# Block product as three float32r terms, with the transposed x1 split by ScalarE and VectorE

## The chip, the cores and the metric

The program runs on one core of a Trainium2 chip. Its engines are TensorE (PE; its weight loads are shown apart as PEld), VectorE (DVE), ScalarE (ACT), GpSimd (POOL) and SyncE (SP, which only starts transfers here). Each engine works through its own queue in order, and the engines meet at semaphores. The metric is the device time of one execution in microseconds (us); lower is better.

## What is computed

For each of 128 batches (128 tokens of 256 features), a layer norm is followed by cross attention with 16 heads against a context, a residual sum (x1), a second layer norm, and a feed-forward step in which a router keeps 96 of the 128 tokens and sends them through one 256x256 matrix and a gelu.

```python
def attn(q_in, ctx):                     # 16 heads of 16
    q = q_in @ Wq + bq
    k, v = split(ctx @ Wkv + bkv)
    return (softmax(q @ k.T / 4) @ v) @ Wo + bo
x1 = x + attn(layernorm(x), ctx)         # x: [128, 128, 256], float32
h = layernorm(x1)
score = h @ w_router                     # top 96 of 128 tokens in each batch
out = x1 + where(token is kept, gelu(h @ w_block), h)
```

## The kernel before

**Tiling.** One batch is one tile of 128 tokens on 128 partitions, so each of the 128 steps of the main loops handles one batch per stage. The code is written engine by engine, with the order of every queue written out by hand. Several batches are in flight: in step s, PE computes the scores of batch s, transposes the inputs of batch s+5, and runs the block product (h @ w_block and the router column together, `w_z_sb`, 258 columns) of batch s-4.

**PE, step s** (loop at the end of the tensor block): `scores(s)`, `transpose_inputs(s+5)`, `values(s-1)`, queries or keys of a later pair, on two steps of eight a small router transpose, `projection(s-2)`, `block_product(s-4)`, `transpose_x1(s-3)`, `attention(s-1)`. The weight matrices for q, k and v stand as a float32r high part and a low part, and `three_terms` multiplies them as hi·hi + hi·lo + lo·hi (six matmuls of 256 columns for two halves of the contraction). `projection` and `block_product` go through `full_terms`: two float32 matmuls, each of which the trace shows as two records.

**ACT, step s**: `attention_copy(s-2)` (PSUM to `o_sb`, 256 columns), `gelu_tanh(s-7)`, `inputs_high(s+5)` (the 512-column cast of the transposed inputs to float32r, L578), then the exponentials of batch s in the order j = 3, 2, 1, 0. Each j is four ACTIVATEs of 128 columns with an accumulated sum, so a batch has sixteen, each followed by a record that reads the accumulator.

**DVE, step s**: `x1_transposed(s-4)` (copy of the transposed x1 from PSUM to `xt_sb`, L721), layer-norm statistics, router steps, `maxima(s, 3)` and `(s, 2)`, value bias, `inputs_low`, reciprocal of the sums, `maxima(s, 1)`, query or key bias, residual sum, `maxima(s, 0)`, the final sum of an older batch, and `product_scaled(s-4)`, which reads the block product.

**What ties them.** `scores(s)` waits until ACT has done j = 1 of batch s-1 (`exp_ready[1]`), because they share PSUM banks; only the bank of j = 0 alternates. `inputs_high(s+5)` waits for the transposes behind `scores(s)` (`t_mm`). The exponentials (s, j) wait for the maxima (s, j), and these for the scores. `values(s-1)` waits for `attention_copy(s-2)`. The transposed x1 lies in the bank that queries and keys use next (`ps_q`), and those wait for the copy out of it (`xt_ready`).

**The tail.** After the last step the remaining batches drain. There ACT also does five `unprocessed` steps in a row (L602, batches B-13 to B-9), and DVE runs `gelu_product(B-5)`, which needs ACT's tanh of that batch, ahead of `product_scaled(B-2)`.

Of the kernel before, what the change touches and what calls it, by code (L numbers as in the profile page):

```python
# [6 lines left out]
def cross_attention_routed_ffn(  # L7
# [14 lines left out]
    f32 = mybir.dt.float32  # L22
    f32r = mybir.dt.float32r
# [7 lines left out]
    P = 128  # L31
# [16 lines left out]
    with ctx:  # L48
        def sb(name, shape, dt=f32):
            return ctx.enter_context(nc.sbuf_tensor(name, shape, dt))  # L50

        def sem(name):
            return ctx.enter_context(nc.semaphore(name))
# [14 lines left out]
        x1_sb = sb("x1_sb", [P, R, E])  # L68
        xt_sb = sb("xt_sb", [P, 2, E])
        z_sb = sb("z_sb", [P, R, ZW])  # L70
# [3 lines left out]
        w_o_sb = sb("w_o_sb", [P, C, E])  # L74
        w_z_sb = sb("w_z_sb", [P, C, ZW])
        bq_sb = sb("bq_sb", [P, C])
        bk_sb = sb("bk_sb", [P, C])
# [56 lines left out]
        def has(b):  # L134
            return 0 <= b < B

        def upto(b):
            return min(b + 1, B)
# [17 lines left out]
        w_lo_ready = {n: sem(f"w_{n}_lo_ready") for n in "qkv"}  # L156
        w_mean_mm, w_z_ready = sem("w_mean_mm"), sem("w_z_ready")
        st1_ready, mv1_ready, ve1_ready, rstd1_ready = sem("st1_r"), sem("mv1_r"), sem("ve1_r"), sem("rstd1_r")
        st2_ready, mv2_ready, ve2_ready, rstd2_ready = sem("st2_r"), sem("mv2_r"), sem("ve2_r"), sem("rstd2_r")
# [21 lines left out]
        x1_ready = sem("x1_ready")  # L181
        xt_mm = sem("xt_mm")
        xt_ready = sem("xt_ready")
        z_mm = sem("z_mm")
# [93 lines left out]
        def _(pe):  # L278
# [17 lines left out]
            def full_terms(dst, lhs, rhs):  # L296

                for c in range(C):
                    last = nc.tensor.matmul(dst, lhs(c), rhs(c), start=(c == 0), stop=(c == C - 1))  # L299
                return last  # L300
# [123 lines left out]
            def block_product(b, settled=False):  # L424

                if not has(b):
                    return
                if not settled:
                    pe.wait_ge(xt_ready, upto(b))
                pe.wait_ge(t_lo_ready, upto(b + 9))  # L430
                if has(b - 1) and not has(b + 9):
                    pe.wait_ge(z_ready, upto(b - 1))
                full_terms(ps_z,
                           lambda c: xt_sb[:, b % 2, c * T:(c + 1) * T],
                           lambda c: w_z_sb[:, c, :]).then_inc(z_mm, 1)

# [114 lines left out]
        def _(act):  # L551
# [4 lines left out]

            def exps(b, j, settled=False):

                if not has(b):
                    return  # L560
                act.wait_ge(max_ready[j], upto(b))
                if j == 3 and has(b - 4) and not settled:
                    act.wait_ge(a_mm, upto(b - 4))
                for c in range(C):
                    for par in range(2):
                        h = c * 2 * J + 2 * j + par
                        last = nc.scalar.activation(e_sb[:, b % 4, j, c, par, :], ps_s[:, bank(b, j), c, par, :], ACT.Exp,  # L567
                                                    bias=neg_max[:, b % 4, h:h + 1],
                                                    accum_out=sums[:, b % 4, h:h + 1])
                last.then_inc(exp_ready[j], 1)  # L570

# [73 lines left out]
            exps(1, 1)  # L645
            exps(1, 0)

            for s in range(2, B):
                sure = 20 <= s < B - 1
                attention_copy(s - 2, sure)  # L650
                gelu_tanh(s - 7)
                inputs_high(s + 5, sure)
                exps(s, 3, sure)
                exps(s, 2)
                exps(s, 1)
                exps(s, 0)

            attention_copy(B - 2)
            gelu_square(B - 5)
            gelu_tanh(B - 7)  # L660
            gelu_square(B - 4)
            attention_copy(B - 1)
            gelu_tanh(B - 6)
            for b in range(B - 13, B - 8):
                unprocessed(b)
# [12 lines left out]
        def _(dve):  # L678
# [35 lines left out]

            def x1_transposed(b, settled=False):

                if has(b):
                    dve.wait_ge(xt_mm, upto(b))
                    if has(b - 2) and not settled:
                        dve.wait_ge(z_mm, upto(b - 2))  # L720
                    nc.vector.tensor_copy(xt_sb[:, b % 2, :], ps_xt).then_inc(xt_ready, 1)  # L721

# [190 lines left out]
            for s in range(2, B):  # L913
                sure = 20 <= s < B - 1
                x1_transposed(s - 4, sure)
                if s >= 4:
# [35 lines left out]
            router(B - 16, 8)  # L952
            x1_transposed(B - 4)
            aggregate2(B - 3)
            router(B - 16, 9)
            inverse_sums(B - 1)
            router(B - 16, 10)
            x1_transposed(B - 3)
            product_scaled(B - 4)
# [5 lines left out]
            final(B - 15)  # L965
            x1_transposed(B - 2)
            gelu_product(B - 6)
# [3 lines left out]
            product_scaled(B - 3)  # L971
            x1_transposed(B - 1)
            final(B - 14)
# [236 lines left out]
```

## Time and profile before

| | |
|---|---|
| three runs, us | 920.46, 921.12, 921.23 (median 921.12) |
| profiled execution: its span, first to last instruction | 919.4 us |
| median of the runs less that span | 1.7 us |
| busy share of the span: PE, PEld, DVE, ACT, POOL | 97%, 82%, 95%, 96%, 87% |
| mean DMA rate | 77 GB/s |

The page gives the span of one profiled execution; what lies around it is the 1.7 us by which the median of the other runs is longer. Busy shares are averages: three engines are above 94%, so they do not say by themselves which one sets the pace. For that one reads a single batch in the timeline, engine beside engine, and looks for who starts right behind whom.

### The profile page before, as it was taken

To read this page: it belongs to the slowest core of one execution; us is meant where nothing else is said; L and a number is where in the kernel's file an instruction comes from. 1 tells how busy PE (TensorE), PEld (TensorE's weight loads), DVE (VectorE), ACT (ScalarE), POOL (GpSimd) and SP (SyncE) were. 2 spreads that over 40 slices of the span, in tenths; PEclk is the share of its full clock that TensorE was granted. 3 is DMA by queue.
4 is the path that set the end of the run, shared out by engine and by line. 5 is a ranking of instruction groups with operands and counts; after the bars stand their busy time and mean duration, and the time that the engine had idled before them with its cause. 6 is when DMAs were issued, how large, how long until landed. Compare 5 with 4: busy or idle time off the path is not lost. (4 is left out here: it accounts for less than half of the span.)

```text
span 919.4 us, 31003 instructions
## 1 busy us (share of the span) xinstructions
PE 889.4 (97%) x10306; PEld 753.9 (82%) x10306; DVE 873.5 (95%) x2320; ACT 879.5 (96%) x4503; POOL 796.8 (87%) x1488
## 2 busy tenths in 40 slices
PE   7899999999999999999999999999999999999973
PEld 6788888888888888888888888888888888888861
DVE  6899999999999999999999999999999999999887
ACT  5999999999999999999999999999999999999983
POOL 4568789999989999899999999999899999998865
PEclk9999999999999999999999999999999999999997
DMA  6222123223223223223223223223223222221102
GB/s 198 62 65 71 46 61 95 57 84 93 57 84 95 60 83 92 58 86 91 70 75 91 59 86 91 71 74 89 76 71 89 76 71 87 76 61 53 49 24 92
DMA packets 70976, 70.45 MB, mean 77 GB/s; under 512 B 12064, under 2 KB 62752, under 8 KB 70816
## 3 DMA queue, kind: packets, MB, share of 16 engines
q1 hardware_dynamic: 69456, 67.68, 25.5%
q8 instruction: 82, 1.34, 0.6%
q10 hardware_dynamic: 1360, 0.79, 0.3%
q14 instruction: 78, 0.64, 0.2%
HBM read 35.13 MB, written 16.78 MB: 56 GB/s over the span
## 5 line engine op out<-in xcount | busy, mean ns | idle before, releaser
L567 ACT ACTIVATE e_sb<-ps_s,neg_max 128x128 f32<-128x128 f32 x2048 | 719.1, 411 | 4.4 <-DVE neg_max L712 3.9
L567 ACT ACTIVATION_READ_ACCUMULATOR e_sb<-ps_s,neg_max 128x1 f32 x2048 | 513.5, 251 | 0.0
L712 DVE TENSOR_REDUCE neg_max<-ps_s 128x4 f32<-128x512 f32 x512 | 329.0, 663 | 26.4 <-PE ps_s L337 26.4
L337 PE MATMUL ps_s<-q_eo,k_sb 32*128 32x256 f32 x2048 | 146.6, 400 | 1.1 <-DVE k_sb L790 0.5
L402 PE MATMUL ps_a<-e_sb,v_pad 128*32 128x128 f32 x4096 | 138.4, 276 | 2.2 <-DVE x_sb L729 1.6
L299 PE MATMUL ps_a<-w_o_sb,o_sb 128*128 128x256 f32 x512 | 133.2, 382 | 2.0 <-DVE v_sb L803 1.9
L299 PE MATMUL ps_t<-w_z_sb,xt_sb 128*128 128x258 f32 x512 | 132.6, 381 | 1.3 <-DVE z_sb L815 1.3
L1042 POOL TENSOR_TENSOR v_pad<-v_sb,recip 128x256 f32<-128x256 f32 x128 | 79.6, 622 | 54.0 <-DVE recip L757 52.5
L402 PEld LDWEIGHTS ps_a<-e_sb,v_pad 128*32 128x32 f32 x4096 | 104.1, 109 | 24.0 <-issue 21.6
L337 PEld LDWEIGHTS ps_s<-q_eo,k_sb 32*128 32x128 f32 x2048 | 92.5, 184 | 29.4 <-ACT e_sb L567 17.0
L1031 POOL TENSOR_TENSOR x_sb<-x_sb,bo_sb 128x256 f32<-128x256 f32 x128 | 114.0, 892 | 0.2
L299 PEld LDWEIGHTS ps_t<-w_z_sb,xt_sb 128*128 128x128 f32 x512 | 97.3, 191 | 15.4 <-issue 1.8
L299 PEld LDWEIGHTS ps_a<-w_o_sb,o_sb 128*128 128x128 f32 x512 | 88.0, 189 | 10.1 <-issue 2.4
L1088 POOL TENSOR_TENSOR g_sb<-g_sb,z_sb 128x256 f32<-128x256 f32 x128 | 90.9, 710 | 0.3
L578 ACT CAST t_hi<-ps_t 128x512 fp32r<-128x512 f32 x126 | 74.2, 589 | 14.0 <-PE ps_t L366 10.5
L764 DVE TENSOR_TENSOR t_lo<-ps_t,t_hi 128x512 fp32r<-128x512 f32 x126 | 85.2, 676 | 1.4 <-ACT t_hi L578 1.4
L292 PE MATMUL ps_a<-w_v_hi,t_hi 128*128 128x256 f32 x256 | 84.4, 330 | 1.7 <-ACT o_sb L586 1.6
L1102 POOL TENSOR_TENSOR z_sb<-g_sb,z_sb 128x256 f32<-128x256 f32 x121 | 82.8, 685 | 0.0
L1071 POOL TENSOR_TENSOR g_sb<-z_sb 128x256 f32<-128x256 f32 x123 | 75.6, 614 | 0.3 <-DVE z_sb L815 0.3
L292 PE MATMUL ps_q<-t_hi,w_k_hi 128*128 128x256 f32 x252 | 71.2, 282 | 1.6 <-DVE q_raw L777 1.6
L292 PE MATMUL ps_a<-w_v_lo,t_hi 128*128 128x256 f32 x256 | 72.5, 283 | 0.0
L292 PE MATMUL ps_q<-t_hi,w_q_hi 128*128 128x256 f32 x256 | 72.3, 282 | 0.2 <-DVE t_lo L764 0.2
(102 smaller groups left out, 2197.6 us busy)
## 6 DMA issues: line engine op xcount, KB each, us to landing
x_sb<-in_x SPq DMA_DIRECT2D x64, 256.0 KB, 2.9
c_sb<-in_ctx SPq DMA_DIRECT2D x64, 256.0 KB, 3.1
out<-z_sb SPq DMA_DIRECT2D x64, 256.0 KB, 2.4
q_eo<-q_raw SPq DMA_DIRECT2D x504, 32.0 KB, 2.0
z_sb<-in_L_xattn_Wkv ACTq DMA_DIRECT2D x2, 256.0 KB, 7.2
z_sb<-in_L_xattn_Wq ACTq DMA_DIRECT2D x1, 256.0 KB, 4.5
w_z_sb<-in_L_ffn_w_block SPq DMA_DIRECT2D x1, 256.0 KB, 7.6
w_o_sb<-in_L_xattn_Wo SPq DMA_DIRECT2D x1, 256.0 KB, 7.0
```

The source lines that it names most:

```text
L292: last = nc.tensor.matmul(dst, lhs(a, c), rhs(b, c), start=(c == 0 and n == 0), stop=(c == C - 1 and n == len(terms) - 1))
L299: last = nc.tensor.matmul(dst, lhs(c), rhs(c), start=(c == 0), stop=(c == C - 1))
L337: mm = nc.tensor.matmul(ps_s[:, bank(b, j), c, :, :], k_sb[rows, r2, c, h * T:(h + 1) * T], q_eo[rows, r2, :, c, h, :], start=True, stop=True)
L402: mm = nc.tensor.matmul(ps_attn[32 * j:32 * j + 32, c * T:(c + 1) * T], v_pad[:, b % 2, c * J + j, par:par + 2, :].rearrange("p a d -> p ( ...
L567: last = nc.scalar.activation(e_sb[:, b % 4, j, c, par, :], ps_s[:, bank(b, j), c, par, :], ACT.Exp, bias=neg_max[:, b % 4, h:h + 1], accu ...
L712: nc.vector.tensor_reduce(neg_max[:, b % 4, :].rearrange("p (c j q) -> p j c q", c=C, j=J)[:, j, :, :], ps_s[:, bank(b, j), :, :, :], AX.X ...
L764: nc.vector.tensor_tensor(t_lo[part].rearrange("p k c t -> p (k c) t"), inputs_bank(b)[:, :].rearrange("p (n t) -> p n t", t=T), t_hi[part ...
L1031: nc.gpsimd.tensor_tensor(x_sb[:, b % R, :], x_sb[:, b % R, :], bo_sb[:, :], ALU.add).then_inc(xb_ready, 1)
L1042: nc.gpsimd.tensor_tensor(v_pad[:, b % 2, :, 0:3:2, :], v_sb[:, b % 2, :].rearrange("p (g q d) -> p g q d", q=2, d=D), recip[:, b % 4, :]. ...
L1071: nc.gpsimd.tensor_tensor(g_sb[:, b % 4, :], z_sb[:, b % R, 0:E], z_sb[:, b % R, 0:E], ALU.mult).then_inc(square_ready, 1)
L1088: nc.gpsimd.tensor_tensor(g_sb[:, b % 4, :], g_sb[:, b % 4, :], z_sb[:, b % R, 0:E], ALU.mult).then_inc(cubic_ready, 1)
L1102: nc.gpsimd.tensor_tensor(z_sb[:, b % R, 0:E], g_sb[:, b % 4, :], z_sb[:, b % R, 0:E], ALU.mult).then_inc(gelu_ready, 1)
```

## The change

The block product goes from `full_terms` to `three_terms`: six float32r matmuls instead of two float32 ones. For that, both operands need a high and a low part. The weights are split once (`block_weights_high` on ACT in step 2, `block_weights_low` on DVE in step 3). The transposed x1 is split in every batch: ACT writes the high part with a new copy (`x1_high`, PSUM to float32r, 256 columns), and DVE subtracts it from PSUM to get the low part (`x1_low`), where it made a plain copy before. `x1_high(s-4)` stands on ACT between j = 1 and j = 0 of batch s-1, and `attention_copy(s-2)` moves from behind those last four exponentials to between their two halves. The diff shows PE's queue first, then ACT's, then DVE's.

```diff
             def block_product(b, settled=False):
...
-                full_terms(ps_z,
-                           lambda c: xt_sb[:, b % 2, c * T:(c + 1) * T],
-                           lambda c: w_z_sb[:, c, :]).then_inc(z_mm, 1)
+                if b == 0:
+                    pe.wait_ge(w_z_lo_ready, 1)
+                three_terms(ps_z,
+                            lambda a, c: (xt_hi, xt_lo)[a][:, b % 2, c * T:(c + 1) * T],
+                            lambda a, c: (w_z_hi, w_z_lo)[a][:, c, :]).then_inc(z_mm, 1)
...
+            def block_weights_high():
+
+                act.wait_ge(w_z_ready, 1)
+                nc.scalar.copy(w_z_hi[:, :, :], w_z_sb[:, :, :]).then_inc(w_z_hi_ready, 1)
+
+            def x1_high(b, settled=False):
+
+                if has(b):
+                    act.wait_ge(xt_mm, upto(b))
+                    nc.scalar.copy(xt_hi[:, b % 2, :], ps_xt).then_inc(xt_hi_ready, 1)
...
-            exps(1, 0)
 
             for s in range(2, B):
                 sure = 20 <= s < B - 1
+                x1_high(s - 4, sure)
+                exps(s - 1, 0, halves=(0,))
                 attention_copy(s - 2, sure)
+                exps(s - 1, 0, halves=(1,))
                 gelu_tanh(s - 7)
                 inputs_high(s + 5, sure)
                 exps(s, 3, sure)
                 exps(s, 2)
                 exps(s, 1)
-                exps(s, 0)
-
+                if s == 2:
+                    block_weights_high()
+
+            x1_high(B - 4)
+            exps(B - 1, 0, halves=(0,))
             attention_copy(B - 2)
+            exps(B - 1, 0, halves=(1,))
+            x1_high(B - 3)
             gelu_square(B - 5)
             gelu_tanh(B - 7)
             gelu_square(B - 4)
             attention_copy(B - 1)
+            x1_high(B - 2)
             gelu_tanh(B - 6)
-            for b in range(B - 13, B - 8):
+            unprocessed(B - 13)
+            unprocessed(B - 12)
+            x1_high(B - 1)
+            for b in range(B - 11, B - 8):
                 unprocessed(b)
...
-            def x1_transposed(b, settled=False):
-
-                if has(b):
-                    dve.wait_ge(xt_mm, upto(b))
-                    if has(b - 2) and not settled:
-                        dve.wait_ge(z_mm, upto(b - 2))
-                    nc.vector.tensor_copy(xt_sb[:, b % 2, :], ps_xt).then_inc(xt_ready, 1)
+            def block_weights_low():
+
+                dve.wait_ge(w_z_hi_ready, 1)
+                nc.vector.tensor_tensor(w_z_lo[:, :, :], w_z_sb[:, :, :], w_z_hi[:, :, :].bitcast(f32),
+                                        ALU.subtract).then_inc(w_z_lo_ready, 1)
+
+            def x1_low(b):
+
+                if has(b):
+                    dve.wait_ge(xt_hi_ready, upto(b))
+                    nc.vector.tensor_tensor(xt_lo[:, b % 2, :], ps_xt, xt_hi[:, b % 2, :].bitcast(f32),
+                                            ALU.subtract).then_inc(xt_ready, 1)
...
-                x1_transposed(s - 4, sure)
+                x1_low(s - 4)
+                if s == 3:
+                    block_weights_low()
```

In the tail of DVE's queue each `x1_transposed(b)` is replaced in its place by `x1_low(b)`.

On ACT, in the middle of the run, this is how one batch's last exponentials stood before, with the waits of each instruction (`e_sb` are the exponentials, `o_sb` the attention output, `g_sb` the gelu's work tile, `t_hi` the inputs' high part):

```order
L567 ACTIVATE e_sb,sums<-ps_s,neg_max 128x128 [waits max_ready1]
L567 ACTIVATE e_sb,sums<-ps_s,neg_max 128x128 x3
L567 ACTIVATE e_sb,sums<-ps_s,neg_max 128x128 [waits max_ready0]
L567 ACTIVATE e_sb,sums<-ps_s,neg_max 128x128 x3
L586 COPY o_sb<-ps_a 128x256 [waits a_mm]
L609 ACTIVATE g_sb<-g_sb 128x256 [waits cubic_ready]
L578 CAST t_hi<-ps_t 128x4x128 [waits t_mm]
```

and this is how they stand now (`xt_hi` is the high part of the transposed x1):

```order
L586 ACTIVATE e_sb,sums<-ps_s,neg_max 128x128 [waits max_ready1]
L586 ACTIVATE e_sb,sums<-ps_s,neg_max 128x128 x3
L573 CAST xt_hi<-ps_q 128x256 [waits xt_mm]
L586 ACTIVATE e_sb,sums<-ps_s,neg_max 128x128 [waits max_ready0]
L586 ACTIVATE e_sb,sums<-ps_s,neg_max 128x128
L606 COPY o_sb<-ps_a 128x256 [waits a_mm]
L586 ACTIVATE e_sb,sums<-ps_s,neg_max 128x128 x2
L629 ACTIVATE g_sb<-g_sb 128x256 [waits cubic_ready]
L598 CAST t_hi<-ps_t 128x4x128 [waits t_mm]
```

One instruction of 256 columns came in ahead of the last four exponentials, and the COPY of `o_sb` moved up by two of them.

On DVE, between two steps, from the statistics of x1 to the first maximum of the next batch, before:

```order
L735 BN_STATS st<-x_sb 128x6 [waits x1_ready]
L815 TENSOR_SCALAR z_sb<-ps_t,rstd 128x258 [waits stored2,z_mm]
L721 COPY xt_sb<-ps_q 128x256 [waits xt_mm]
L746 BN_STATS st<-x_sb 128x6
L740 BN_AGGR mv<-st 128x2 [waits st2_r]
L751 BN_AGGR mv<-st 128x2 [waits st1_r]
L712 TENSOR_REDUCE neg_max<-ps_s 128x2x2 [waits s_mm3]
```

and now:

```order
L771 BN_STATS st<-x_sb 128x6 [waits x1_ready]
L851 TENSOR_SCALAR z_sb<-ps_t,rstd 128x258 [waits stored2,z_mm]
L756 TENSOR_TENSOR xt_lo<-ps_q,xt_hi 128x256 [waits xt_hi_ready]
L782 BN_STATS st<-x_sb 128x6
L776 BN_AGGR mv<-st 128x2 [waits st2_r]
L787 BN_AGGR mv<-st 128x2 [waits st1_r]
L743 TENSOR_REDUCE neg_max<-ps_s 128x2x2 [waits s_mm3]
```

The instruction stands in the same place, but its input now comes from ACT as well (`xt_hi_ready`), where it waited for PE alone (`xt_mm`).

On ACT in the tail, from the last exponentials on, before:

```order
L567 ACTIVATE e_sb,sums<-ps_s,neg_max 128x128 x3
L586 COPY o_sb<-ps_a 128x256 [waits o_mm,a_mm]
L595 ACTIVATE g_sb<-z_sb 128x256 [waits gelu_ready,z_ready]
L609 ACTIVATE g_sb<-g_sb 128x256 [waits cubic_ready]
L595 ACTIVATE g_sb<-z_sb 128x256 [waits gelu_ready,z_ready]
L586 COPY o_sb<-ps_a 128x256 [waits o_mm,a_mm]
L609 ACTIVATE g_sb<-g_sb 128x256 [waits cubic_ready]
L602 ACTIVATE x_sb<-x_sb,beta,alpha 128x256 [waits xt_mm,beta_ready] x5
L609 ACTIVATE g_sb<-g_sb 128x256 [waits cubic_ready]
L595 ACTIVATE g_sb<-z_sb 128x256 [waits gelu_dve_ready,z_ready]
```

and now:

```order
L586 ACTIVATE e_sb,sums<-ps_s,neg_max 128x128 x2
L573 CAST xt_hi<-ps_q 128x256 [waits xt_mm]
L615 ACTIVATE g_sb<-z_sb 128x256 [waits gelu_ready,z_ready]
L629 ACTIVATE g_sb<-g_sb 128x256 [waits cubic_ready]
L615 ACTIVATE g_sb<-z_sb 128x256 [waits gelu_ready,z_ready]
L606 COPY o_sb<-ps_a 128x256 [waits o_mm,a_mm]
L573 CAST xt_hi<-ps_q 128x256 [waits xt_mm]
L629 ACTIVATE g_sb<-g_sb 128x256 [waits cubic_ready]
L622 ACTIVATE x_sb<-x_sb,beta,alpha 128x256 [waits xt_mm,beta_ready] x2
L573 CAST xt_hi<-ps_q 128x256 [waits xt_mm]
L622 ACTIVATE x_sb<-x_sb,beta,alpha 128x256 [waits xt_mm,beta_ready] x3
L629 ACTIVATE g_sb<-g_sb 128x256 [waits cubic_ready]
```

Three of the new copies stand in this stretch, the last of them ahead of three of the five `unprocessed` steps and of the gelu work behind these.

## Rows read from the trace of the kernel before

**Rows 1.** The page's part 1: busy time (share of the span) and instructions of each engine.

```profile
PE 889.4 (97%) x10306; PEld 753.9 (82%) x10306; DVE 873.5 (95%) x2320; ACT 879.5 (96%) x4503; POOL 796.8 (87%) x1488
```

**Rows 2.** Groups by line, ACT: form, count, busy us, mean ns, idle before, releaser.

```profile
L578 ACT CAST t_hi<-ps_t 128x512 fp32r<-128x512 f32 x126 | 74.2, 589 | 14.0 <-PE ps_t L366 10.5
...
L586 ACT COPY o_sb<-ps_a 128x256 f32<-128x256 f32 x128 | 60.2, 470 | 2.2 <-PE ps_a L402 2.2
```

**Rows 3.** Timeline, ACT, one batch: start us, us, line, operation, out<-in.

```profile
502.24 0.26 ACT L567 ACTIVATION_READ_ACCUMULATOR e_sb<-ps_s,neg_max 128x1 f32 x1
...
503.61 0.29 ACT L567 ACTIVATION_READ_ACCUMULATOR e_sb<-ps_s,neg_max 128x1 f32 x1
503.70 0.46 ACT L586 COPY o_sb<-ps_a 128x256 f32<-128x256 f32 x1
503.95 0.52 ACT L609 ACTIVATE g_sb<-g_sb 128x256 f32<-128x256 f32 x1
504.57 0.59 ACT L578 CAST t_hi<-ps_t 128x512 fp32r<-128x512 f32 x1
...
505.31 0.20 ACT L567 ACTIVATION_READ_ACCUMULATOR e_sb<-ps_s,neg_max 128x1 f32 x1
...
510.45 0.31 ACT L567 ACTIVATION_READ_ACCUMULATOR e_sb<-ps_s,neg_max 128x1 f32 x1
```

**Rows 4.** Timeline, PE, the same batch: start us, us, line, operation, matmul records.

```profile
502.80 1.15 PE L337 MATMUL ps_s<-q_eo,k_sb 32*128 32x256 f32 x16
...
504.15 0.38 PE L366 MATMUL ps_t<-ident,c_sb 128*128 128x128 f32 x2
...
505.10 0.28 PE L292 MATMUL ps_q<-t_hi,w_q_hi 128*128 128x256 f32 x1
...
506.52 1.03 PE L299 MATMUL ps_a<-w_o_sb,o_sb 128*128 128x256 f32 x4
507.39 1.04 PE L299 MATMUL ps_t<-w_z_sb,xt_sb 128*128 128x258 f32 x4
508.26 0.38 PE L382 MATMUL ps_q<-ident,x_sb 128*128 128x128 f32 x2
508.57 1.08 PE L402 MATMUL ps_a<-e_sb,v_pad 128*32 128x128 f32 x32
509.58 1.15 PE L337 MATMUL ps_s<-q_eo,k_sb 32*128 32x256 f32 x16
```

**Rows 5.** Timeline, ACT, the batch before: tanh and cast with nothing between.

```profile
497.25 0.53 ACT L609 ACTIVATE g_sb<-g_sb 128x256 f32<-128x256 f32 x1
497.65 0.60 ACT L578 CAST t_hi<-ps_t 128x512 fp32r<-128x512 f32 x1
```

**Rows 6.** Line 586 in two stretches: count, durations in ns, first and last start us.

```profile
L586 ACT COPY o_sb<-ps_a x116: 454/473/487, 65.0 to 853.9; 128x256 f32<-128x256 f32 x116
...
L586 ACT COPY o_sb<-ps_a x6: 373/462/477, 860.7 to 893.8; 128x256 f32<-128x256 f32 x6
```

**Rows 7.** Groups by line, DVE: residual sum from PSUM, and the copy of transposed x1.

```profile
L729 DVE TENSOR_TENSOR x_sb<-ps_a,x_sb 128x256 f32<-128x256 f32 x128 | 53.3, 416 | 2.9 <-PE ps_a L299 1.9
...
L721 DVE COPY xt_sb<-ps_q 128x256 f32<-128x256 f32 x128 | 52.4, 409 | 0.1
```

**Rows 8.** Timeline, DVE, the batch of rows 3: copy of x1, then two maxima.

```profile
503.15 0.40 DVE L721 COPY xt_sb<-ps_q 128x256 f32<-128x256 f32 x1
...
504.22 1.25 DVE L712 TENSOR_REDUCE neg_max<-ps_s 128x4 f32<-128x512 f32 x2
```

**Rows 9.** Timeline, the tail after the last exponentials: ACT, PE, DVE.

```profile
899.69 2.55 ACT L602 ACTIVATE x_sb<-x_sb,beta,alpha 128x256 f32<-128x256 f32 x5
...
901.37 0.38 PE L382 MATMUL ps_q<-ident,x_sb 128*128 128x128 f32 x2
...
902.83 0.42 DVE L821 SCALAR_TENSOR_TENSOR z_sb<-g_sb,z_sb 128x256 f32<-128x256 f32 x1
903.48 0.49 DVE L815 TENSOR_SCALAR z_sb<-ps_t,rstd 128x258 f32<-128x258 f32 x1 [0.24 <-PE ps_t L299]
```

More of the change, by code:

```diff
@@ L68, in cross_attention_routed_ffn @@
         x1_sb = sb("x1_sb", [P, R, E])
-        xt_sb = sb("xt_sb", [P, 2, E])
+        xt_hi = sb("xt_hi", [P, 2, E], f32r)
+        xt_lo = sb("xt_lo", [P, 2, E], f32r)
         z_sb = sb("z_sb", [P, R, ZW])
@@ L75, in cross_attention_routed_ffn @@
         w_z_sb = sb("w_z_sb", [P, C, ZW])
+        w_z_hi = sb("w_z_hi", [P, C, ZW], f32r)
+        w_z_lo = sb("w_z_lo", [P, C, ZW], f32r)
         bq_sb = sb("bq_sb", [P, C])
@@ L157, in cross_attention_routed_ffn @@
         w_mean_mm, w_z_ready = sem("w_mean_mm"), sem("w_z_ready")
+        w_z_hi_ready, w_z_lo_ready = sem("w_z_hi_ready"), sem("w_z_lo_ready")
         st1_ready, mv1_ready, ve1_ready, rstd1_ready = sem("st1_r"), sem("mv1_r"), sem("ve1_r"), sem("rstd1_r")
@@ L182, in cross_attention_routed_ffn @@
         xt_mm = sem("xt_mm")
+        xt_hi_ready = sem("xt_hi_ready")
         xt_ready = sem("xt_ready")
@@ L555, in weights_high, with exps @@
                                      scale=SCALE if n == "q" else 1.0).then_inc(w_hi_ready[n], 1)
-            def exps(b, j, settled=False):
+            def block_weights_high():
[5 more added lines that the diff above has]
+                    nc.scalar.copy(xt_hi[:, b % 2, :], ps_xt).then_inc(xt_hi_ready, 1)
+            def exps(b, j, settled=False, halves=range(C)):
                 if not has(b):
                     return
[L561 to L564, printed above, removed]
+                if 0 in halves:
+                    act.wait_ge(max_ready[j], upto(b))
+                    if j == 3 and has(b - 4) and not settled:
+                        act.wait_ge(a_mm, upto(b - 4))
+                for c in halves:
                     for par in range(2):
@@ L569, in exps @@
                                                     accum_out=sums[:, b % 4, h:h + 1])
-                last.then_inc(exp_ready[j], 1)
+                if C - 1 in halves:
+                    last.then_inc(exp_ready[j], 1)
             def inputs_high(b, settled=False):
@@ L952, in _ @@
             router(B - 16, 8)
-            x1_transposed(B - 4)
+            x1_low(B - 4)
             aggregate2(B - 3)
@@ L957, in _ @@
             router(B - 16, 10)
-            x1_transposed(B - 3)
+            x1_low(B - 3)
             product_scaled(B - 4)
@@ L965, in _ @@
             final(B - 15)
-            x1_transposed(B - 2)
+            x1_low(B - 2)
             gelu_product(B - 6)
@@ L971, in _ @@
             product_scaled(B - 3)
-            x1_transposed(B - 1)
+            x1_low(B - 1)
             final(B - 14)
```

## The prediction

> **What bounds the kernel now.** The page comes first: PE is busy for 97% of the span, ACT for 96%, DVE for 95% [rows 1]. That names three candidates, so I read one batch in the timeline, engine beside engine.
>
> On PE the rows are packed. The block product starts at 507.39 and the next instruction at 508.26; the transposes of x1 follow, the attention product at 508.57 runs for 1.08 us, and the next batch's scores start at 509.58, just before its modelled end [rows 4]. From one start of the scores to the next are 6.78 us, and there is no gap in them.
>
> On ACT the rows look as dense, but one start is late. The transposes of the inputs end at 504.15 + 0.38 = 504.53 on PE [rows 4], and the cast of those inputs starts at 504.57 on ACT [rows 3]. The tanh ahead of it had started at 503.95, so cast follows tanh by 0.62 us. In the batch before it followed by only 0.40 [rows 5]. The cast is the place where ACT waits for PE, and the group of the cast shows the same: it carries nearly all the idle time of ACT's repeated groups, 14.0 us, with the transposes as the releaser [rows 2]. The recorded idle understates the wait, because without it an instruction starts before its predecessor has ended. So PE sets the pace and ACT has some room. How much room decides this change.
>
> I take ACT's own need from ends, since an engine cannot finish work faster than it does it. Between the accumulator reads that end at 502.50 and 503.90 lie four exponentials, 0.35 us each; between those that end at 505.51 and 510.76 lie fifteen in 5.25 us, the same [rows 3]. The copy ends 0.26 after the last of them (504.16), the tanh 0.31 after the copy (504.47) [rows 3]. The cast, when not held, ends 0.47 after the tanh (498.25 against 497.78) [rows 5]. Sum: 16 x 0.35 + 0.26 + 0.31 + 0.47 = 6.64; with a hundredth or two of rounding in each term I use **6.67 us** per batch (6.64 to 6.70). The measured pace is (853.9 - 65.0) / 115 = **6.86 us** [rows 6]. ACT's room is 0.19 us per batch.
>
> **The change part by part.**
>
> *PE.* The block product takes 507.39 to 508.26, 0.87 us [rows 4]. The new form is six float32r matmuls. Twelve such matmuls, those of the queries, take 505.10 to 506.52, 0.118 us each [rows 4], so six take 0.71; if changing over costs up to 0.08 us, 0.79. PE gains 0.08 to 0.16 us per batch; I take 0.12, hence a PE pace near 6.74. The new ones have 258 columns, where the trace has 256 for float32r; I go by that nearest row.
>
> *ACT, the new copy.* `x1_high` moves 256 columns out of PSUM. Its nearest row is the attention copy, the same size from the same memory: 0.26 us from end to end, and 0.25 from its start to the next start [rows 3]. The input cast, which also writes float32r, takes 0.47 for twice the columns [rows 5], so the output type adds nothing visible. I take 0.27, with 0.25 and 0.30 as ends. It needs `xt_mm`: those transposes end at 508.64 [rows 4], and the next point at which ACT has done j = 1 is about 502.50 + 6.8 = 509.3 [rows 3], so it does not wait.
>
> The Trainium skill ("ScalarE: Activation LUTs", section "What ACT_TABLE_LOAD costs") gives an ACTIVATE with immediate operands 186 ns + 0.833 ns per column, with about 93 ns of overlap between neighbours; an estimate from it is 0.306 us for 256 columns. The trace's copy is shorter; by the page's figure the sum below would come out some 4 us higher.
>
> So ACT needs 6.67 + 0.27 = **6.94 us** per batch, more than the 6.86 of today. The room is used up, and ACT becomes the bound, at +0.08 us per batch.
>
> *ACT, the moved copy.* `attention_copy` comes earlier by two exponentials and later by the new copy. It costs the same where it is; it waits for the attention product of batch s-2, which ended just as the scores began, at about 502.85, against a new place near 502.50 + 0.27 + 0.70 = 503.47 [rows 3, 4]. What it releases, the values on PE, stands behind the transposes. No cost, no gain.
>
> *Does PE stay out of the way?* Count from T, the end of j = 1 (502.50). ACT then does the new copy, two exponentials, the attention copy, two exponentials and the tanh: 0.27 + 0.70 + 0.26 + 0.70 + 0.31 = 2.24, and only then the cast. PE had the transposes ready at T + 2.03 (504.53) [rows 3, 4]. So PE's part of the loop has 0.2 us to spare, and PE now waits at the scores.
>
> *DVE.* The subtraction replaces the copy. The residual sum, also one PSUM and one SBUF operand of 256 columns, takes 416 ns against 409 for the copy [rows 7]: nothing. The wait is new. Queued behind it on DVE are statistics, a router step and the maxima of j = 3, for which the exponentials of j = 3 wait. The copy started at T + 0.65 (503.15) [rows 8]; the high part is there at about T + 0.3. The first of two maxima starts at 504.22 and takes half of 1.25 us [rows 8], so it is done by T + 2.4; the exponentials need it at T + 2.24 + 0.47 = T + 2.7. Cover of 0.3 us; if it were gone, each 0.1 us would cost about 12 us over the run.
>
> *Weights split once.* About 0.5 us on ACT and 0.7 on DVE in steps 2 and 3, where ACT has neither tanh nor x1 yet. In steps 4 to 6, still without tanh, ACT keeps room and PE's gain may show. I put the start at 0 +- 1 us.
>
> *Tail.* The last transposes of x1 end at 901.75 [rows 9]; `x1_high(B-1)` cannot start before, and now three of the five `unprocessed` stand behind it (2.55 / 5 = 0.51 each [rows 9]). They end near 901.75 + 0.3 + 1.53 = 903.6, the tanh behind them near 904.0, `gelu_product(B-5)` on DVE near 904.4 instead of its start at 902.83 and end at 903.25, and `product_scaled(B-2)`, queued behind it, starts near 904.4 instead of 903.48 [rows 9]. That chain leads to the last router, so about +1.0 us.
>
> **Sum.** 115 batches x 6.94 = 798.1, against 853.9 - 65.0 = 788.9 [rows 6]: +9.2 us. One more interval with a cast (860.7 - 853.9 = 6.8) gains +0.1. The next five have no cast, so ACT needs 6.94 - 0.47 = 6.47 against (893.8 - 860.7) / 5 = 6.62 [rows 6]: -0.8 at best. Tail +1.0, start 0. Together **+9.5 us**: a span of 919.4 + 9.5 = 928.9, and, with the 1.7 us by which the median of the runs exceeds the profiled span, **930.6 us**. The ends of the ACT terms (6.64 + 0.25 to 6.70 + 0.30) would be 6.89 to 7.00, that is 925 to 937.
>
> **The rivals.**
>
> *Faster: the copy hides in the wait before the cast.* If `x1_high` costs clearly less than ACT's 0.19 us of room, PE stays the bound and its 0.12 us per batch come through. It decides at an ACT pace under 6.84, a copy below 0.17. All of PE's gain would be 6.86 - 0.12: about 14 us off and 1 us tail, 908 us; half of it 915. For it: the cast does wait. Against: no 256-column ACT instruction in the trace ends less than 0.26 after its predecessor [rows 3]. Chance 0.06.
>
> *Same: starts, not ends, are ACT's rate.* The reads start 1.37 us apart over four exponentials, 0.343 each [rows 3]. By starts ACT needs 16 x 0.343 + 0.25 + 0.40 + 0.48 = 6.62, and with the copy's 0.25 just 6.87, the pace of today: 920 to 922.9. Against: the read takes 0.20 at the batch's first exponential and 0.31 at its last [rows 3], so starts only run ahead of ends. Chance 0.09.
>
> *Slower still: a new hand-over.* DVE's or PE's cover of 0.2 to 0.3 us is used up, by the wait for the high part or because a PE that waits for the exponentials starts late; at 0.1 us beyond the cover 12 us more, 942, and 936 to 955 in all. Chance 0.05.
>
> *Slower still: ACT is the bound already.* PE's busy rows are modelled at their ends, and PEld is busy for only 82% [rows 1]. If PE has slack today, the whole 0.27 us comes on top in 121 intervals: +33, some 954 us. Against: the cast starts 0.04 us behind the transposes [rows 3, 4]. Chance 0.02. The Trainium skill ("Perfetto Trace Analysis", section "Identifying the Most-Contended Engine") tells to judge TensorE by the busy share of its weight loads and not of its matmuls, which speaks for this rival. Here the timeline speaks against that reading: PE issues without a gap.
>
> **How the numbers follow.** The forecast, ACT at 6.89 to 7.00 per batch, has 0.78: 925 to 937, most likely 930.6. Alone that is short of 8 in 10, so the range goes down to 921.5, which takes in about half of the case of no change, and up to 938, which takes in the start of the new hand-over. Left out are the faster case (0.06), the other half of no change (0.04 to 0.05), most of the hand-over (0.04) and the last rival (0.02), together 0.17. A measurement here tells about 0.2%, 1.8 us, from no change. Slower by more: 0.78 + 0.05 + 0.02 = 0.85; same 0.09; faster 0.06.
>
> **What would show it.** Right: the cast's idle time goes to about zero; copy to copy the pace is an even 6.94, also in the router's batches; PE has waits of some 0.2 us per batch at the scores for the exponentials; the new cast's group has 128 instructions of 0.4 to 0.5 us; the block product's six records advance by 0.12 us. Wrong: the cast still starts right behind the transposes (PE bound, faster); ACT shows idle time ahead of the exponentials of j = 3 (DVE late); the exponentials advance by less than 0.35 us from end to end (same).

## The result, and the profile after

The changed kernel takes **929.65 us** (928.42 to 929.73, four runs), the kernel before beside it 921.17 (920.46 to 921.65): ratio 1.0087 [1.0075, 1.0099], so 0.9% slower. The forecast was 930.6. The profiled execution of the changed kernel is the shortest of its four, with a span of 926.6 us.

Two views say most of it. The first gives the busy time of each engine in the steady stretch, from the first to the last of the usual attention copies. Columns: window in us, its length, then busy us (instructions) of PE, PEld, DVE, ACT, POOL, the granted clock of PE, DMA share and GB/s. Before:

```profile
65.00:854.00 789.00, 789.00 (x9232) 671.34 (x9228) 767.62 (x2045) 779.13 (x4028) 717.71 (x1333) 1.00 0.26 75
```

After:

```profile
64.00:860.00 796.00, 776.03 (x9469) 671.85 (x9462) 774.66 (x2049) 796.00 (x4147) 716.96 (x1335) 1.00 0.26 75
```

Before, PE was busy for all of it and ACT had idle time; after, ACT is busy for all of it and PE has 20 us idle. The bound has moved from PE to ACT. The page's part 4, the chain that ended last, after, says the same by engine (before, that chain breaks off after some 3% of the span, so there is nothing to set beside it):

```profile
ACT 93%; PE 2%; issue 2%; DVE 1%; POOL 1%; DMA 0%; POOLq 0%; DVEq 0%; ACTq 0%
```

The second view is one batch on ACT, after (start us, us, line, operation). Its ends are what counts:

```profile
500.65 0.90 ACT L598 CAST t_hi<-ps_t 128x512 fp32r<-128x512 f32 x1
...
505.16 0.59 ACT L586 ACTIVATION_READ_ACCUMULATOR e_sb<-ps_s,neg_max 128x1 f32 x1
505.25 0.76 ACT L573 CAST xt_hi<-ps_q 128x256 fp32r<-128x256 f32 x1
...
506.11 0.61 ACT L586 ACTIVATION_READ_ACCUMULATOR e_sb<-ps_s,neg_max 128x1 f32 x1
506.20 0.78 ACT L606 COPY o_sb<-ps_a 128x256 f32<-128x256 f32 x1
...
507.05 0.64 ACT L586 ACTIVATION_READ_ACCUMULATOR e_sb<-ps_s,neg_max 128x1 f32 x1
507.15 0.85 ACT L629 ACTIVATE g_sb<-g_sb 128x256 f32<-128x256 f32 x1
507.57 0.90 ACT L598 CAST t_hi<-ps_t 128x512 fp32r<-128x512 f32 x1
```

From the end of the first cast (501.55) twelve exponentials end at 505.75, 0.35 us each; then the new copy takes 0.26, two exponentials 0.71, the moved copy 0.26, two exponentials 0.71, the tanh 0.31, the cast 0.47: 6.92 us from cast to cast, without a hole. Over the steady stretch the pace is the same. Line 606 in the steady stretch, after (count, durations in ns, first and last start):

```profile
L606 ACT COPY o_sb<-ps_a x116: 470/781/793, 63.8 to 859.0; 128x256 f32<-128x256 f32 x116
```

That is (859.0 - 63.8) / 115 = 6.915 us per batch against 6.860 [rows 6].

On PE, after, the wait has the predicted size (timeline; in brackets the idle time before and what ended it):

```profile
502.61 1.03 PE L304 MATMUL ps_a<-w_o_sb,o_sb 128*128 128x256 f32 x4
503.28 0.47 PE L297 MATMUL ps_t<-w_z_hi,xt_hi 128*128 128x258 f32 x1
...
504.07 0.28 PE L297 MATMUL ps_t<-w_z_lo,xt_hi 128*128 128x258 f32 x1
504.19 0.38 PE L387 MATMUL ps_q<-ident,x_sb 128*128 128x128 f32 x2
504.50 1.08 PE L407 MATMUL ps_a<-e_sb,v_pad 128*32 128x128 f32 x32
505.80 1.15 PE L342 MATMUL ps_s<-q_eo,k_sb 32*128 32x256 f32 x16 [0.22 <-ACT e_sb L586]
...
507.15 0.38 PE L371 MATMUL ps_t<-ident,c_sb 128*128 128x128 f32 x2
507.29 0.37 PE L297 MATMUL ps_a<-w_v_hi,t_hi 128*128 128x256 f32 x1
```

Projection and block product together take 504.19 - 502.61 = 1.58 us, before 508.26 - 506.52 = 1.74 [rows 4]: PE saves 0.16 and then stands for 0.22 at the scores. The groups of the cast, the moved copy and the new copy, after (columns as in [rows 2]):

```profile
L598 ACT CAST t_hi<-ps_t 128x512 fp32r<-128x512 f32 x126 | 109.4, 868 | 3.3 <-PE ps_t L371 3.3
...
L606 ACT COPY o_sb<-ps_a 128x256 f32<-128x256 f32 x128 | 93.8, 733 | 2.6 <-PE ps_a L407 2.6
L573 ACT CAST xt_hi<-ps_q 128x256 fp32r<-128x256 f32 x128 | 91.0, 711 | 1.5 <-PE ps_q L387 1.5
```

The idle time before the cast fell from 14.0 us [rows 2] to 3.3, while its mean rose from 589 to 868 ns. The cast did not become slower: its record starts early and ends when its turn comes. The exponentials, with the same 0.35 us from end to end, show it too, before and then after:

```profile
L567 ACT ACTIVATE e_sb<-ps_s,neg_max 128x128 f32<-128x128 f32 x2048 | 719.1, 411 | 4.4 <-DVE neg_max L712 3.9
```

```profile
L586 ACT ACTIVATE e_sb<-ps_s,neg_max 128x128 f32<-128x128 f32 x2048 | 818.3, 684 | 2.7 <-DVE neg_max L743 2.7
```

Where the time is, section by section in the two profiled executions:

| stretch | before, us | after, us | difference | forecast |
|---|---|---|---|---|
| start, to the first of these copies | 65.0 | 63.8 | -1.2 | 0 |
| 115 steady batches | 788.9 | 795.2 | +6.3 | +9.2 |
| the next six intervals, to batch B-2 | 39.9 | 39.8 | -0.1 | -0.7 |
| batch B-2 to B-1 | 5.3 | 6.7 | +1.4 | |
| last attention copy to the end | 20.3 | 21.1 | +0.8 | +1.0 |

### The profile page after: what moved, and what is told of

It reads as the page before. It is cut to its first block, busy times and chain, and to the rows that moved or that the text cites. A ratio compares the mean times of both kernels' runs of the same rounds, so it can differ in the third digit from the quotient of the medians.

```text
span 926.6 us, 31626 instructions
## 1 busy us (share of the span) xinstructions
PE 874.7 (94%) x10562; PEld 754.9 (81%) x10562; DVE 881.3 (95%) x2321; ACT 899.1 (97%) x4632; POOL 795.6 (86%) x1488
## 4 chain that ended last, share of the span: by engine, by line
ACT 93%; PE 2%; issue 2%; DVE 1%; POOL 1%; DMA 0%; POOLq 0%; DVEq 0%; ACTq 0%
ACT e_sb L586 77%; ACT t_hi L598 6%; ACT o_sb L606 4%; ACT g_sb L629 4%; ACT xt_hi L573 3%; PE ps_a L304 1%; PE ps_q L297 0%; DMA x_sb<-in_x 0%; PE ps_s L342 0%; PE ps_t L297 0%; DVE z_sb L904 0%; DVE neg_max L743 0%; PE ps_a L407 0%; ACT q_eo L637 0%; PE ps_t L371 0%
## 5 line engine op out<-in xcount | busy, mean ns | idle before, releaser
L586 ACT ACTIVATE e_sb<-ps_s,neg_max 128x128 f32<-128x128 f32 x2048 | 818.3, 684 | 2.7 <-DVE neg_max L743 2.7
L586 ACT ACTIVATION_READ_ACCUMULATOR e_sb<-ps_s,neg_max 128x1 f32 x2048 | 774.6, 524 | 0.0
L598 ACT CAST t_hi<-ps_t 128x512 fp32r<-128x512 f32 x126 | 109.4, 868 | 3.3 <-PE ps_t L371 3.3
L629 ACT ACTIVATE g_sb<-g_sb 128x256 f32<-128x256 f32 x128 | 101.6, 794 | 1.4 <-POOL g_sb L1126 1.4
L297 PE MATMUL ps_t<-w_z_hi,xt_hi 128*128 128x258 f32 x256 | 96.7, 378 | 2.2 <-DVE z_sb L851 2.2
L606 ACT COPY o_sb<-ps_a 128x256 f32<-128x256 f32 x128 | 93.8, 733 | 2.6 <-PE ps_a L407 2.6
L573 ACT CAST xt_hi<-ps_q 128x256 fp32r<-128x256 f32 x128 | 91.0, 711 | 1.5 <-PE ps_q L387 1.5
```

The lines of the kernel that those rows point to most:

```text
L297: last = nc.tensor.matmul(dst, lhs(a, c), rhs(b, c), start=(c == 0 and n == 0), stop=(c == C - 1 and n == len(terms) - 1))
L573: nc.scalar.copy(xt_hi[:, b % 2, :], ps_xt).then_inc(xt_hi_ready, 1)
L598: nc.scalar.copy(t_hi[:, n, :, :, h * T:(h + 1) * T].rearrange("p k c t -> p (k c) t"), inputs_bank(b)[:, :].rearrange("p (n t) -> p n t", ...
L606: nc.scalar.copy(o_sb[:, b % 2, :], ps_attn).then_inc(o_ready, 1)
L629: nc.scalar.activation(g_sb[:, b % 4, :], g_sb[:, b % 4, :], ACT.Tanh, scale=SLOPE).then_inc(tanh_ready, 1)
```

## The experiments

Ratios are to the kernel before, measured beside each run on the same chip, with 95% intervals. Not all runs had the same chip (the kernel before takes 920.2 to 921.2 us on them), so runs are best compared by their ratios. Code names are those of the changed kernel.

**The two halves apart.** First PE's part alone: three terms on PE, one plain copy of the transposed x1 on DVE, ACT as before.

```diff
-    lambda a, c: (xt_hi, xt_lo)[a][:, b % 2, c * T:(c + 1) * T],
+    lambda a, c: (xt_hi, xt_hi)[a][:, b % 2, c * T:(c + 1) * T],
...
-                x1_high(s - 4, sure)
...
-                    nc.vector.tensor_tensor(xt_lo[:, b % 2, :], ps_xt, xt_hi[:, b % 2, :].bitcast(f32),
-                                            ALU.subtract).then_inc(xt_ready, 1)
+                    nc.vector.tensor_copy(xt_hi[:, b % 2, :], ps_xt).then_inc(xt_ready, 1)
```

> The three-term block product alone: DVE copies the transposed x1 out of PSUM once, as before, now into the float32r tile; ACT has no new copy and its old order. The low part of x1 is left out (the high part stands in for it), so that ACT and DVE do what they did before. Theory (PE set the pace before, ACT needs 6.67 us and DVE 6.72 us per batch): PE falls from 6.86 to about 6.74 per batch, so 115 x 0.12 = 14 us less, 906 to 911 us. Rival, that ACT or the loop through ACT was the bound already: no change, 919 to 923 us.

Measured 914.39 us, 0.9925 [0.9913, 0.9938]: less time, as the theory had it, but about half of the gain and outside the 906 to 911 expected. Then ACT's and DVE's part alone, with the old product:

```diff
-    three_terms(ps_z,
+    full_terms(ps_z,
...
-    nc.vector.tensor_tensor(xt_lo[:, b % 2, :], ps_xt, xt_hi[:, b % 2, :].bitcast(f32), ALU.subtract)...
+    nc.vector.tensor_copy(xt_sb[:, b % 2, :], ps_xt)...
```

> The new ACT copy alone: ACT and DVE stand as in the changed kernel (DVE waits for the high part, then copies x1), PE multiplies in full float32 as before and the high part is not used. Theory (ACT bound at 6.92 per batch, PE's 6.86 no longer shows): 929 to 934 us, the time of the changed kernel or little above it. Rival, that the faster product pays for a part of the copy in the changed kernel: 0.12 x 115 = 14 us more than it, about 943 us. Rival, that the copy hides and the loss lies elsewhere: 921 us.

Measured 930.44, 1.0099 [1.0086, 1.0113]. With the old, longer product the time is that of the changed kernel: once ACT is the bound, PE's saving is worth nothing that can be told from the noise. This run also has the wait on DVE and the moved copy; the runs on these two, below, show no loss from either, so the loss is the new copy's. PE's saving alone is worth 6.6 us; why not more, the later runs show in part.

**The price of the copy.** The new copy is made twice, first into a scratch tile.

```diff
+    nc.scalar.copy(xt_more[:, b % 2, :], ps_xt)
     nc.scalar.copy(xt_hi[:, b % 2, :], ps_xt).then_inc(xt_hi_ready, 1)
```

> The new ACT copy twice per batch (the first into a scratch tile). Theory (ACT has no room left in the changed kernel): the second copy shows in full, 0.26 to 0.27 us x 124 = 32 to 34 us on top of the changed kernel, 961 to 964 us, where the first one cost only 8 us. Rival, that the loss comes from the wait or the order and ACT still has room: well under 945 us.

Measured 964.36, 1.047 [1.0455, 1.0484]. In the timeline of ACT, doubled copy, the two stand thus:

```profile
503.29 1.04 ACT L574 CAST xt_more<-ps_q 128x256 fp32r<-128x256 f32 x1
503.55 1.06 ACT L575 CAST xt_hi<-ps_q 128x256 fp32r<-128x256 f32 x1
```

Their ends, 504.33 and 504.61, are 0.28 apart. The first copy, without PE's saving, cost 9 us (the run above); the same copy again costs 34.7. The first fell mostly into the room that ACT had; for the second none was left.

**The wait on DVE.** DVE's input comes from `x1_sb`, so that it no longer waits for ACT; PE waits for the high part instead.

```diff
-    dve.wait_ge(xt_hi_ready, upto(b))
-    nc.vector.tensor_tensor(xt_lo[:, b % 2, :], ps_xt, xt_hi[:, b % 2, :].bitcast(f32), ALU.subtract)...
+    dve.wait_ge(x1_ready, upto(b))
+    if has(b - 2):
+        dve.wait_ge(z_mm, upto(b - 2))
+    nc.vector.tensor_copy(xt_lo[:, b % 2, :], x1_sb[:, b % R, :])...
```

> The changed kernel without DVE's wait for ACT's high part: DVE copies x1 from its SBUF tile into the place of the low part, so the subtraction is left out; PE's queries and keys wait for ACT's copy instead. Theory (DVE's wait of some 0.1 us per batch is covered): 928 to 931 us. Rival, that the new wait on DVE delays the maxima and by them the exponentials: DVE's waits for the high part, 13.9 us in all in the changed kernel, come back, 916 to 924 us.

Measured 930.01, 1.0094 [1.0081, 1.0108]. The time stays, so the wait was covered, as the forecast had it; no wait of PE for the high part shows in this trace that could have taken its place.

**The moved copy.** In the changed kernel the attention copy goes back behind all four exponentials; then, in the kernel before, it alone is moved.

```diff
     x1_high(s - 4, sure)
-    exps(s - 1, 0, halves=(0,))
+    exps(s - 1, 0)
     attention_copy(s - 2, sure)
-    exps(s - 1, 0, halves=(1,))
```

> The changed kernel with the attention copy back behind all four last exponentials (both in the loop and after it). Theory (the moved copy costs ACT the same wherever it stands, and PE has 0.2 us per batch to spare for the later values): 929 to 931 us. Rival, that the move is what keeps the loss small (PE would wait for the later copy and ACT for PE in turn): 0.1 us or more per batch on top, over 940 us.

Measured 936.62, 1.0165 [1.0151, 1.0179]: 7 us worse than the changed kernel. That is outside the theory's range and short of the rival's, but it has the rival's direction. The waits of this run (engine and tile, for whom; us, times, longest):

```profile
PEld ps_a L297 <- ACT o_sb L606: 36.6, 110, 1.2
```

In nearly every batch PE's weight load for the values stands until the attention copy is done; PE's matmuls themselves show 8.4 us in 33 waits for it. For the kernel before, the opposite edit:

```diff
-                exps(s, 0)
+                exps(s - 1, 0, halves=(0,))
                 attention_copy(s - 2, sure)
+                exps(s - 1, 0, halves=(1,))
```

> The kernel before with only the attention copy moved between the two halves of the last exponentials; no new copy, no three terms. Theory (the copy costs ACT the same wherever it stands and PE did not wait for it before): no change, 919 to 923 us. Rival, that the earlier copy frees PE's values by itself, as putting it back cost 7 us in the changed kernel: 914 us.

Measured 918.01, 0.9976 [0.9966, 0.9986] (eight runs): a small gain, just outside the 919 to 923 expected. The trace of before shows where it lies. Timeline, before, PE and ACT, one batch:

```profile
497.00 0.46 ACT L586 COPY o_sb<-ps_a 128x256 f32<-128x256 f32 x1
...
497.24 0.38 PE L366 MATMUL ps_t<-ident,c_sb 128*128 128x128 f32 x2
...
497.51 0.39 PE L292 MATMUL ps_a<-w_v_hi,t_hi 128*128 128x256 f32 x1
```

The same place, two steps ahead of the router's longest, with the copy moved:

```profile
494.62 0.45 ACT L588 COPY o_sb<-ps_a 128x256 f32<-128x256 f32 x1
...
495.53 0.38 PE L366 MATMUL ps_t<-ident,c_sb 128*128 128x128 f32 x2
...
495.67 0.36 PE L292 MATMUL ps_a<-w_v_hi,t_hi 128*128 128x256 f32 x1
```

Before, the values start 0.27 us behind the transposes, 0.05 after the copy has ended (497.46); with the copy moved, they start 0.14 behind them, as in the next step of the kernel before, where the copy was done in time. From start to start of the scores, eight steps in a row read so (each row from its own first step):

| | step lengths, us |
|---|---|
| before | 6.78 6.93 6.79 7.13 6.78 6.80 6.78 6.91 |
| copy moved, nothing else | 6.79 6.78 6.79 7.13 6.77 6.77 6.78 6.89 |
| PE's part alone | 6.89 6.79 6.71 7.08 6.63 6.77 6.65 6.87 |
| the change | 6.91 6.92 6.92 6.92 6.98 6.85 6.92 6.91 |
| the change, copy back | 7.02 6.88 7.08 6.91 7.29 6.63 7.06 6.92 |

Moving the copy takes 0.15 us from one step in eight and a little from others, 0.024 per batch. The row of PE's part alone suggests why its gain stayed at 6.6 us: its shortest steps are down at ACT's own 6.64, the long ones, with the router's work, hardly moved, and the copy holds the values more often than before. Waits of PEld for `o_sb` over the whole run (us, times, longest), before and then with PE's part alone:

```profile
PEld ps_a L292 <- ACT o_sb L586: 4.0, 7, 0.9
```

```profile
PEld ps_a L295 <- ACT o_sb L598: 7.1, 22, 0.9
```

How much each of the three takes was not measured apart.

**The tail.** The last `x1_high` moves behind the five `unprocessed` steps, the tanh of B-5 and the square of B-3, and `x1_low(B-1)` behind `gelu_product(B-5)`.

```diff
-            x1_high(B - 1)
             for b in range(B - 11, B - 8):
                 unprocessed(b)
             gelu_tanh(B - 5)
             gelu_square(B - 3)
+            x1_high(B - 1)
```

> The changed kernel with ACT's last new copy (batch 127) behind all five unprocessed steps, the tanh of batch 123 and one square, and DVE's subtraction behind the gelu product of batch 123. Theory (the last new copy held these up and, through the gelu product on DVE, the chain to the last router): from the last attention copy to the end 20.3 us as before the change in place of 21.1, some 0.8 us less, 928 to 929.5 us. Rival, that the tail's loss is elsewhere: 21.1 us stay.

Measured 927.87, 1.0086 [1.0072, 1.0100]; the ratio is that of the changed kernel. From the last attention copy (906.4) to the end (927.5) it takes 21.1 us, as without the edit, and the scaled product of the last batch starts 7.2 us after that copy in both (6.3 before). `product_scaled(B-2)` did come 0.35 us earlier behind that copy (4.73 in place of 5.08), and the tanh of B-4 too. But the gelu product of B-4, behind two more steps on DVE, took that up again. Without the edit and then with it (start us, us):

```profile
912.14 0.61 DVE L857 SCALAR_TENSOR_TENSOR z_sb<-g_sb,z_sb 128x256 f32<-128x256 f32 x1
```

```profile
912.71 0.94 DVE L855 SCALAR_TENSOR_TENSOR z_sb<-g_sb,z_sb 128x256 f32<-128x256 f32 x1
```

It is longer by 0.33 us and ends 7.3 behind the copy in both; why it is longer is not shown. So this order alone does not set the 0.8 us. Other traces narrow it a little: from the last attention copy to the end it takes 20.3 us with the moved copy alone, 20.8 with PE's part alone and some 21.2 with ACT's and DVE's part alone. Each half lengthens the tail by itself, and the two do not add up; what in them costs the time stays open.

**A share of the batches.** If ACT's room is 0.19 us and a copy costs 0.27, only some batches should take the new form. All of these contain the moved copy. Odd batches first:

```diff
+        def split(b):
+            return b % 2 == 1
...
-                if has(b):
+                if has(b) and split(b):
                     act.wait_ge(xt_mm, upto(b))
```

(PE takes `three_terms` or `full_terms`, DVE the subtraction or the copy, by the same test.)

> Half of each: odd batches take the changed form (ACT copy, DVE subtraction, three terms), even batches the old one (DVE copy, full float32). Theory (two engines with averages of their own and some tenths of a us of cover between them): ACT 6.67 + 0.27/2 = 6.80, PE 6.86 - 0.12/2 = 6.80 per batch, so 6.80 to 6.84, 914 to 920 us, less than both kernels. Rival, that each batch pays its own slower engine: 6.92 and 6.86 in turn, 6.89, about 924 us.

Measured 916.96, 0.9956 [0.9942, 0.9969]. Every fourth batch, those whose product falls into the router's long steps:

```diff
-            return b % 2 == 1
+            return b % 4 == 0
```

> Three terms only for batches 0, 4, 8, ..., whose block product stands in the steps in which PE also has a router transpose (7.06 and 7.14 us before); the others as before. Theory (averages count): PE 6.86 - 0.16/4 = 6.82, ACT 6.67 + 0.27/4 = 6.74, so PE stays the bound at 6.82, 916 to 918 us. Rival, that only the long steps gain and the gain is not handed on: 6.86 in the others' mean stays, 919 to 921 us.

Measured **914.91**, 0.9936 [0.9922, 0.9949], less than either kernel and a little less than expected. Then the even batches (`b % 2 == 0`), the other fourth (`b % 4 == 2`) and three of eight (`b % 8 in (0, 2, 4)`):

> Three terms for even batches, so again in the steps with a router transpose, full float32 for odd ones. Same averages as with odd batches (ACT 6.80, PE 6.78), where 6.82 was measured; if it matters that PE's gain falls on its long steps, 6.79 to 6.81, 912 to 916 us; if a batch with both a long PE step and the ACT copy pays for both, over 917 us, the time with odd batches.

Measured 916.41, 0.9954 [0.9941, 0.9966], between the two branches.

> Three terms for batches 2, 6, 10, ..., a quarter of all as in the run with every fourth, but now in steps without a router transpose. If only the number counts (averages, passed on through the cover between the engines): 914 to 916 us again. If it counts that PE's gain falls on its long steps: 917 to 920 us.

Measured 917.99, 0.9981 [0.9972, 0.9990].

> Three terms for batches 0, 2 and 4 of every eight. By averages ACT needs 6.67 + 0.27 x 3/8 = 6.77 and PE 6.86 - 0.16 x 3/8 = 6.80: between the run with a quarter (6.81 measured) and that with the even half (6.83 measured), 913 to 917 us. Under 913 us would mean that the balance of ACT and PE was still the limit; 914 to 917 us that DVE, at 6.72 by its own work, or the coupling of the engines within a batch is.

Measured 916.33, 0.9957 [0.9944, 0.9969]. The right yardstick is the moved copy alone, 918.0 (0.9976). Against it the fourth in the router's steps gains 3.1 us (by the ratios 3.7) and the other fourth nothing, though both do the same amount of work. The steps of the former show it: 6.86 6.78 6.78 6.98 6.78 6.78 6.78 6.77. The 7.13 of the router fell to 6.98 and the 6.89 to 6.77, where ACT has most room, while one plain step rose to 6.86; in the 6.78 of the plain steps ACT's need is 6.64, and a copy of 0.27 is more than that leaves. That does not make every plain step worthless: the odd half lies in plain steps alone, and its steady steps are 6.825 us on average against 6.838 with the moved copy alone, 1.4 us over 115 batches; why it gains where the other fourth does not was not settled. More batches than a fourth lost part of the gain again; why three of eight, with ACT idle for 3 us of its 791, is not better was not settled.

## Why the prediction was right

*The bound.* "The room is used up, and ACT becomes the bound" holds: ACT is busy for all 796 us, the pace is even at 6.91 to 6.92 in six steps of eight (6.98 and 6.85 in the other two), and PE stands 0.22 us at the scores. The parts-alone runs show both sides, and the doubled copy its price: 0.27 was forecast, 0.26 to 0.28 measured.

*The mis-sized term.* ACT's need before was 6.64 by the raw sum of ends, and I put "a hundredth or two of rounding in each term" on top of it. 6.915 less the forecast copy's 0.27 is 6.645, and less the 0.26 of the rows 6.655. The sum's 6.94 is 0.025 above the measured pace, 115 x 0.025 = 2.9 us, the difference between +9.2 and the measured +6.3 in the steady stretch. But this is one execution, the shortest of four. Three other traces have the same order on ACT in that stretch: 795.4 us with ACT's and DVE's part alone, 795.2 without DVE's wait, and 861.1 - 63.9 = 797.2 in the run of the tail order, 6.932 per batch or +8.3. So the term was too large by 1 to 3 us, and executions differ by as much.

*PE.* The gain was 0.16 per batch, the upper end of 0.08 to 0.16. As forecast, it has no effect on the time while ACT is the bound.

*The ends.* Rows 5 were read as a cast that does not wait. Its transposes end at 497.24 + 0.38 = 497.62, and it starts at 497.65: right behind them, as the one that waits. What tells the two apart is their ends: the cast of rows 3 ends at 505.16, 0.69 behind the tanh, the one of rows 5 only 0.47, and 0.47 is also what it takes in the changed kernel, where ACT has no idle time. The figure was right; the start beside it did not show it.

*The moved copy* is the step that failed. "What it releases, the values on PE, stands behind the transposes. No cost, no gain" looked at the moved copy against the kernel before, where it comes earlier by only 0.43 us (two exponentials less the new copy). Against the right alternative, the new copy ahead and this one left in place, it comes earlier by two exponentials, and that is worth 7.0 us; and even in the kernel before the copy held the values in some steps. The edit that looked like a detail keeps the loss at 0.9% instead of 1.7%.

*DVE* was as forecast, by the run without the wait. *The start* came out 1.2 us shorter in this execution, and 1.1 shorter in the run of the tail order, but only 0.4 with the DVE wait taken out (64.6); I read nothing from it. *The tail*: +0.8 against +1.0 from the last copy on, but with the named order undone it stayed, so that term was right by luck. The 0.8 us that the five batches without cast were to give back came out as 0.2. Between B-2 and B-1 stand 1.4 us that no term had; they come with the lower clock (below), for in the run of the tail order, where the clock stayed full, the same stretch takes 5.4. Over all +7.2 us in the spans, +8.5 between the medians, +9.5 forecast. Without that 1.4 us, which no term foresaw, the spans would differ by 5.8, so some of the nearness is luck too.

*The signs.* The new copy's group was to show 0.4 to 0.5 us; it shows 0.711, its records being stretched like the others. Another sign was wrong in itself. "The cast still starts right behind the transposes (PE bound, faster)" is what the rows after show: transposes to 507.15 + 0.38 = 507.53, cast at 507.57, the same 0.04 as before [rows 3, 4], although the cast now ends only at 508.47, 0.47 behind the tanh. Read by starts, the change would have had PE as its bound still, and by itself the same 0.04 said nothing for PE in the kernel before either. What speaks for PE there is the 0.69 by ends, and above all the run of PE's part alone. The rival "same" also went by starts and gave 6.87: the steps of 6.92 speak against it. The rival of the faster side falls with the copy's 0.27. "ACT is the bound already" falls with PE's part alone, which gained 6.6 us although PEld was at only 82% [rows 1] and ACT at 96%. The Trainium skill ("Perfetto Trace Analysis", section "Identifying the Most-Contended Engine") judges TensorE's headroom by MFU and by the busy share of its weight loads; by that share ACT would have been the engine to relieve. This kernel's runs do not bear that out (MFU was not worked out here).

## What to carry to other kernels

Before you move work to an engine "with room", add up its need from end to end between two neighbours that never wait, and compare it with the pace; do it step by step, since most of the room may lie in a few long steps, and try the work there first. When an instruction is put into a queue, ask what stands behind it and who waits for that: here moving its neighbour was worth 7 us, beside a loss of 8.5 that remained. And try each half of a change alone: here the half that saved work and the half that cost it had opposite signs.

## What the hardware showed that I had not expected

ACT's records can start soon after their input is there, while the engine is still at work on earlier ones: the cast of the rows after starts at 507.57, the tanh ahead of it ends at 508.00. The exponentials' mean grew from 411 to 684 ns, the cast's from 589 to 868, and the same attention copy reads 473, 781 and 1068 ns (medians) in the kernels before, after and with the copy doubled, while from end to end it takes 0.26 us in all. In this kernel a rising mean on ACT was a sign of a backlog, and the idle time in front of a group said little.

The granted clock of TensorE fell in the tail of the changed kernel's profiled execution. Windows, after (columns as in the first fence):

```profile
895.00:900.00 5.00, 3.11 (x49) 2.67 (x47) 3.76 (x13) 4.62 (x26) 2.90 (x6) 1.00 0.14 52
900.00:905.00 5.00, 4.39 (x38) 3.56 (x42) 3.15 (x10) 1.41 (x4) 3.95 (x9) 0.66 0.01 2
905.00:910.00 5.00, 3.83 (x36) 2.87 (x27) 3.56 (x10) 3.99 (x10) 3.63 (x7) 1.00 0.17 56
```

The clock is full (2.4 GHz) up to about 900, and its mean of 0.66 between 900 and 905 means that the lower of its two levels (1.2 GHz) was granted for some two thirds of that stretch. Ahead of that, PE had been busy for 3.11 of 5 us, with a last wait of 1.28 us for ACT's exponentials. In the timeline of PE, after, the price is on the rows:

```profile
899.98 0.19 PE L495 MATMUL ps_s<-ident,keep_row 8*128 8x8 f32 x1 [1.28 <-ACT e_sb L586]
...
901.88 1.85 PE L304 MATMUL ps_a<-w_o_sb,o_sb 128*128 128x256 f32 x4
```

The projection takes 1.85 us there and 1.03 in the steady stretch, on the path to the last attention copy. In the run of the tail order the same wait of 1.28 us stands ahead of the same transpose, and the clock stayed full. Its window and rows:

```profile
900.00:905.00 5.00, 3.06 (x45) 2.34 (x37) 4.10 (x16) 3.25 (x14) 2.31 (x7) 1.00 0.15 54
```

```profile
902.19 0.20 PE L495 MATMUL ps_s<-ident,keep_row 8*128 8x8 f32 x1 [1.28 <-ACT e_sb L586]
...
903.31 1.03 PE L304 MATMUL ps_a<-w_o_sb,o_sb 128*128 128x256 f32 x4
```

So the wait alone does not decide it, and what does is not shown.
